# Projection to B and C in four column groups of the array, and one transpose of its result

## The chip, the cores and the metric

The kernel runs on one core of a Trainium2 chip. The metric is the device time of one execution in microseconds (us). Three runs of the kernel before took 1530.69, 1531.29 and 1533.32 us; the median is 1531.29 us. Engines are named as the profile names them: PE (TensorE, matmul), PEld (its weight load), DVE (VectorE), ACT (ScalarE), POOL (GpSimd) and SP (the queue that issues DMAs).

## The reference, cut to what matters

The input is x with 2 sequences (B = 2) of 2048 steps and 256 features. A feed-forward layer comes first, then a state-space layer, then the same feed-forward layer again. The change is in the middle layer, in two of its small projections:

```
xc = silu(conv(x_branch))                     # (B, L, 512)
dt = soft_clamp(softplus(xc @ W_dt.T + b_dt))
Bp = xc @ W_B.T                               # (B, L, 16)
Cp = xc @ W_C.T                               # (B, L, 16)
# scan over L: h = h * exp(dt A) + dt * Bp * xc ;  y = sum_n h * Cp + D * xc
```

W_B and W_C have 16 rows each. The kernel keeps them side by side as one matrix `wbc` of 32 columns, so one projection gives 32 numbers a step: 16 of B and 16 of C.

## The kernel before, in words

There are three stages. The pre stage walks over 8 tiles; a tile is 256 steps of both sequences, 512 columns (4 blocks of 128, G = 4, two for each sequence). It runs the first feed-forward layer of the next tile, and the projections and the convolution of the current one, and writes its results to DRAM. The scan stage walks over blocks of 10 steps for both sequences, and the post stage computes the output and the last feed-forward layer.

All work is written out by hand: each engine has its own list, and semaphores tie the lists together. In the pre stage four PSUM banks form a ring. PE fills a bank, ACT reads it, and the list `order` says which result has which place (`fill` on PE, `held` on ACT).

For tile i the lists run as follows.

- PE: `turn_zn(i)` (L346), `project_bc(i-1)` (L369), `project(i, "x")` (L353, after a wait for both ACT copies `copy_z`, L445), `turn_b(i-1)` (L378), `up(i+1)` (L314), `turn_xn(i+2)` (L304), `project(i, "gate")` (L353 again, which needs ring banks that the gelu L432 reads), `down(i+1)` (L328), `project_dt` (L361) with `turn_y(i+1)` (L338) in it.
- ACT: `copy_z` (L445), `copy_bc(i-1)` (L490), `copy_x` (L452), `copy_bt(i-1)` (L987), gelus of tile i+1 (L432), `silu_xc` (L461), `silu_gate` (L469), and softplus and tanh for dt.
- DVE: statistics, `apply1(i+2)` (L582, needs the rstd of POOL L257), the convolution (L642, L645, L650; its first operations need `copy_x`), `split_g(i+1)` (L602, L604), `low_x`, `residual(i+1)` (L612, needs `turn_y(i+1)`), `dt_u`, `apply2`.
- POOL: `norm2(i+1)` (L265 to L277), `spread_b(i-1, 2, 4)` (L1004), `rstd1(i+3)` (L257), then `spread_b(i, 0, 2)` (L995, L997, L1004), which needs `copy_bt`.
- SP: store r (L181), load x (L174), `store_bc` (L187), `store_b` (L1014), store xc, sg, dt and u (L138).

The projection to B and C is computed with the 32 columns of `wbc` as weights. Sequence 0 goes to PSUM partitions 0 to 31 and sequence 1 to partitions 32 to 63, so two groups of 32 array columns are in use. ACT copies the 64 x 256 result to `bcs`. SP stores it to DRAM for the C part, and PE turns it (two transposes of 64 rows) for the B part.

Of the kernel before, what the change touches and what calls it, by code (L numbers as in the profile page):

```python
# [10 lines left out]
ACT = mybir.ActivationFunctionType  # L11
AX = mybir.AxisListType

P = 128
B, L, D = 2, 2048, 256
E = 512
N = 16
H = 1024
TAPS = 4
KD, KE, KH = D // P, E // P, H // P  # L20
TT = 256
TILES = L // TT
G = B * TT // P
# [6 lines left out]
CT = CB * S  # L30
# [20 lines left out]
def pre_stage(nc, dram, w, areas, banks, sem):  # L51
# [7 lines left out]
    own, first, second = areas  # L59
# [19 lines left out]
    xc = second.put("xc", [P, 2, KE, COLS])  # L79
# [1 line left out]
    dt_place = second.offset  # L81
    dt = second.put("dt", [P, KE, COLS])
    u = second.put("u", [P, KE, COLS])
    bcs = second.put("bcs", [B * 2 * N, TT])
    wbc = own.put("wbc", [P, KE, 2 * N])
    convw = own.put("convw", [P, KE, TAPS])
    convb = own.put("convb", [P, KE])
# [19 lines left out]
    ring_done, ring_read = sem("ring_done"), sem("ring_read")  # L107
# [6 lines left out]
    r_out, sg_out, bc_out, dt_out, u_out = (sem(n) for n in ("r_out", "sg_out", "bc_out", "dt_out", "u_out"))  # L114
# [19 lines left out]
    def steps(i):  # L134
        return bass.ds(i * TT, TT)

    def store(sp, name, tile, done, i):
        sp.dma_start(dram[name][:, :, steps(i)],  # L138
                     tile.rearrange("p a (b t) -> p (a b) t", b=B)).then_inc(done, 16)

    def store_dt_u(sp, i):
        sp.wait_ge(dt_ready, i + 1)
        store(sp, "dt", dt[:], dt_out, i)
        sp.wait_ge(u_ready, i + 1)
        store(sp, "u", u[:], u_out, i)
# [23 lines left out]
    def sync(sp, scan, post):  # L169
        def load_x(i, *batches):  # L170
            if i >= XT:
                sp.wait_ge(x1_ready, i - XT + 1)
            for b in batches:
                sp.dma_start(xt[:, i % XT, 2 * b:2 * b + 2, :],  # L174
                             dram["x"][b, steps(i), :].rearrange("(h p) d -> p h d", p=P)
                             ).then_inc(x_in[i % XT], 16)

        def store_r(i):
            sp.wait_ge(r_ready, G * (i + 1))
            for b in range(B):  # L180
                sp.dma_start(dram["r"][b, steps(i), :].rearrange("(h p) d -> p h d", p=P),  # L181
                             r[:, 2 * b:2 * b + 2, :]).then_inc(r_out, 16)

        def store_bc(i):
            sp.wait_ge(ring_read, use["bc", i, 0] + 1)
            for b in range(B):
                sp.dma_start(dram["bc"][:, b, steps(i)], bcs[b * 2 * N:(b + 1) * 2 * N]).then_inc(bc_out, 16)  # L187

        load_x(0, 0)
        sp.dma_start(raw1[:, 0], dram["w1T"][0:P]).then_inc(raw1_in, 16)  # L190
        sp.dma_start(w1n[:, 0:4], dram["w1"][0:H // 2].rearrange("(m p) k -> p m k", p=P)).then_inc(w1n_in, 16)
        load_x(1, 0, 1)
        sp.dma_start(w.b1[:], dram["b1"]).then_inc(b_in, 16)
        sp.dma_start(raw2, dram["w2T"].rearrange("(k p) d -> p k d", p=P)).then_inc(raw2_in, 16)
        sp.dma_start(w.b2[:], dram["b2"]).then_inc(b_in, 16)
        sp.dma_start(w2n, dram["w2"].rearrange("(k p) h -> p k h", p=P)).then_inc(w2n_in, 16)
        for dst, src in ((win[:], dram["winT"].rearrange("(k p) m -> p k m", p=P)),
                         (convw[:], dram["convw"]), (convb[:], dram["convb"]),
                         (normw[:], dram["normw"]), (bdt[:], dram["bdt"]),
                         (wdt[:], dram["wdtT"].rearrange("(k p) m -> p k m", p=P)),  # L200
                         (wbc[:], dram["wbcT"].rearrange("(k p) m -> p k m", p=P))):
            sp.dma_start(dst, src).then_inc(p_in, 16)
        load_x(2, 0, 1)
        sp.wait_ge(pad_zero, 1)
        n = LP - L
        zero = pad[:].rearrange("p a c -> p (a c)")[:, 0:KE * B * n].rearrange("p (a c) -> p a c", c=n)
        sp.dma_start(dram["dt"][:, :, L:LP], zero).then_inc(padded, 16)
        sp.dma_start(dram["u"][:, :, L:LP], zero).then_inc(padded, 16)
        sp.dma_start(dram["bc"][:, :, L:LP], zero[0:2 * N, 0:B, :]).then_inc(padded, 16)
        for b in range(B):  # L210
            sp.dma_start(dram["ub"][b, L:L + S].rearrange("t v x -> (t v) x"),
                         pad[0:S * SPLITS].rearrange("p a c -> p (a c)")[:, 0:ROW]).then_inc(padded, 16)
        store_r(0)
        for i in range(TILES):
            if i + XT < TILES:
                load_x(i + XT, 0, 1)
            if i >= 1:
                store_bc(i - 1)
            if i in (6, 7):
                scan.load_piece(sp, i - 5)  # L220
                for half in range(2):
                    scan.store_piece(sp, i - 6, half)
            if i >= 2:
                scan.store_b(sp, i - 2, 2, G)
            if i >= 1:
                scan.store_b(sp, i - 1, 0, 2)
            sp.wait_ge(xc_ready, 2 * (i + 1))
            store(sp, "xc", xc[:, i % 2], xc_out[i % 2], i)
            sp.wait_ge(ring_read, use["gate", i, KE - 1] + 1)
            store(sp, "sg", sg[:], sg_out, i)  # L230
            if i >= 1:
                store_dt_u(sp, i - 1)
            if i == 4:
                scan.load_piece(sp, 0)
            if i < LAST:
                store_r(i + 1)
            else:
                scan.load_units(sp)
                scan.store_b(sp, LAST - 1, 2, G)
            if i == 3:  # L240
                post.load_params(sp)
                sp.wait_ge(padded, 80)
                scan.load_first(sp)
        store_bc(LAST)

    def gpsimd(pool, scan):
# [46 lines left out]
    def tensor(pe, scan):  # L293
        def fill(what):
            n = use[what]
            if n >= RING:
                pe.wait_ge(ring_read, n - RING + 1)
            return psR[:, n % RING, :]
# [66 lines left out]
        def project_bc(i):  # L365
            out = fill(("bc", i, 0))
            for k in range(KE):
                for b in range(B):
                    mm = pe.matmul(out[b * 2 * N:(b + 1) * 2 * N, 0:TT], wbc[:, k, :],  # L369
                                   xc[:, i % 2, k, b * TT:(b + 1) * TT], start=(k == 0), stop=(k == KE - 1))  # L370
            mm.then_inc(ring_done, 1)

        def turn_b(i):
            out = fill(("bt", i, 0))
            pe.wait_ge(ring_read, use["bc", i, 0] + 1)
            rows = B * 2 * N
            for x in range(TT // P):
                mm = pe.transpose(out[:, x * rows:(x + 1) * rows], bcs[:, x * P:(x + 1) * P], w.ident[0:rows, 0:rows])  # L378
            mm.then_inc(ring_done, 1)

        pe.wait_ge(consts, 1)
        turn_xn(0)
# [8 lines left out]
        for i in range(TILES):  # L391
# [19 lines left out]
            if i in (5, 6):  # L411
                scan.turn_piece(pe, i - 5, psD[:, 0], 0, KE)
        project_bc(LAST)
        turn_b(LAST)

    def scalar(act, scan, post):
        def held(what):
            n = use[what]
            act.wait_ge(ring_done, n + 1)
            return psR[:, n % RING, :]  # L420
# [62 lines left out]
        def copy_bc(i):  # L483
            src = held(("bc", i, 0))
            if i == LAST:
                act.wait_ge(ring_read, use["bc", i, 0])
            if i >= 1:
                act.wait_ge(bc_out, 16 * B * i)
                act.wait_ge(ring_done, use["bt", i - 1, 0] + 1)
            act.activation(bcs[:], src[0:B * 2 * N, 0:TT], ACT.Copy).then_inc(ring_read, 1)  # L490

        def copy_bt(i):
            src = held(("bt", i, 0))
# [288 lines left out]
def scan_stage(nc, dram, w, areas, banks, sem, pre):  # L782
# [9 lines left out]
    own, first, second = areas  # L792
    dtc = own.put("dtc", [P, 2, KE * B, DB * S])
    bc = [own.put(f"bc{q}", [P, B, N, S]) for q in range(RING)]
# [4 lines left out]
    bt = own.put("bt", [P, G, N])  # L799
# [61 lines left out]
    def tile_of(t):  # L861
        return min(t // TT, TILES - 1)
# [1 line left out]


    def relayout(sp, c):
        sp.wait_ge(pre.bc_out, 16 * B * (tile_of((c + 1) * CT) + 1))
        for b in range(B):
            sp.dma_start(
                dram["blk"][c * CB:(c + 1) * CB, b, :, :].rearrange("k n t -> n k t"),  # L870
                dram["bc"][N:2 * N, b, c * CT:(c + 1) * CT].rearrange("n (k t) -> n k t", t=S)
            ).then_inc(blk_out, 16)
# [111 lines left out]
    def copy_bt(act, i, src, read):  # L984
        if i >= 1:
            act.wait_ge(b_split, 2 * i)
        act.activation(bt[:].rearrange("p (b x) n -> p x b n", b=B),  # L987
                       src.rearrange("p (x b n) -> p x b n", b=B, n=2 * N)[:, :, :, 0:N], ACT.Copy).then_inc(read, 1)

    def spread_b(pool, i, q0, q1):  # L990
        if q0 == 0:
# [886 lines left out]
```

## Time and profile before

| | |
|---|---|
| median of 3 runs | 1531.29 us |
| profiled execution, own time | 1536.68 us |
| its span | 1534.8 us |
| PE busy | 1455.1 us (95%) |
| DVE busy | 1255.2 us (82%) |
| ACT busy | 1121.2 us (73%) |
| POOL busy | 939.6 us (61%) |
| pre stage, roughly | 0 to 420 us |
| scan stage, roughly | 420 to 1330 us |
| post stage, roughly | 1330 to 1535 us |

Busy time counts an engine while an instruction of it runs. A row of the timeline gives the start, the time over which a group of instructions ran, the engine and line, what is written and read, the count, and in brackets the idle time before the group and what ended it. A busy share of 95% is a mean over stages; whether a shorter instruction shortens a stage is seen only in the waits of that stage.

### The profile page before, as it was taken

To read this page: it belongs to the slowest core of one execution; us is meant where nothing else is said; L and a number is where in the kernel's file an instruction comes from. 1 tells how busy PE (TensorE), PEld (TensorE's weight loads), DVE (VectorE), ACT (ScalarE), POOL (GpSimd) and SP (SyncE) were. 2 spreads that over 40 slices of the span, in tenths; PEclk is the share of its full clock that TensorE was granted. 3 is DMA by queue.
4 is the path that set the end of the run, shared out by engine and by line. 5 is a ranking of instruction groups with operands and counts; after the bars stand their busy time and mean duration, and the time that the engine had idled before them with its cause. 6 is when DMAs were issued, how large, how long until landed. Compare 5 with 4: busy or idle time off the path is not lost.

```text
span 1534.8 us, 25461 instructions
## 1 busy us (share of the span) xinstructions
PE 1455.1 (95%) x6902; PEld 1020.6 (66%) x6902; DVE 1255.2 (82%) x2526; ACT 1121.2 (73%) x2618; POOL 939.6 (61%) x956
## 2 busy tenths in 40 slices
PE   6999999999979999999999999999999998999998
PEld 5555555555467777777777777777666666677776
DVE  6685566745479999999999999999999998788884
ACT  4444455455999999999999999999999964334243
POOL 0224313432269999999999999999999997400000
PEclk9999999999999999999999999999999999999999
DMA  8215437453757667666666666666545447466420
GB/s 269 83 49 176 131 103 198 139 178 115 233 137 208 169 165 188 168 172 167 172 165 181 177 162 181 157 173 172 133 111 112 95 105 224 116 221 193 150 84 28
DMA packets 231557, 236.28 MB, mean 154 GB/s; under 512 B 46040, under 2 KB 197272, under 8 KB 231416
## 3 DMA queue, kind: packets, MB, share of 16 engines
q1 hardware_dynamic: 230472, 233.34, 54.4%
q8 instruction: 58, 0.95, 0.3%
q10 hardware_dynamic: 944, 1.31, 0.2%
q14 instruction: 83, 0.68, 0.2%
HBM read 136.31 MB, written 98.56 MB: 153 GB/s over the span
## 4 chain that ended last, share of the span: by engine, by line
DVE 35%; POOL 14%; PE 12%; issue 5%; DVEq 1%; POOLq 1%; DMA 1%; ACT 0%; SPq 0%; ACTq 0%
DVE h L1346 22%; POOL rc L1110 13%; DVE banks L1336 8%; PE banks L1495 4%; PE banks L1516 3%; PE banks L1526 3%; DVE qs L1330 2%; PE banks L1170 1%; DVEq L1344 1%; DMA ub<-scratch_ub 1%; DVE q_ln_st L1772 1%; DVE q_g L1681 1%; POOLq L1118 1%; DVE q_x L1653 1%; PE banks L1536 0%
## 5 line engine op out<-in xcount | busy, mean ns | idle before, releaser
L1346 DVE TENSOR_TENSOR_SCAN h<-decay,banks 128x352 f32<-128x352 f32 x820 | 710.4, 882 | 57.4 <-DVE banks L1336 2.9
L1121 POOL TENSOR_TENSOR hc<-h,bc 128x640 f32<-128x640 f32 x410 | 593.3, 1447 | 0.0
L1170 PE MATMUL banks<-hc,w_ident 128*128 128x320 f32 (+1 forms) x1664 | 526.6, 440 | 0.1
L1239 ACT ACTIVATE tb<-dtc,a 128x320 f32<-128x320 f32 (+1 forms) x832 | 417.2, 555 | 4.8 <-DVE x L612 4.8
L1170 PEld LDWEIGHTS banks<-hc,w_ident 128*128 128x128 f32 x1664 | 285.0, 191 | 70.7 <-issue 0.8
L1261 ACT ACTIVATE decay<-tb 128x640 f32<-128x640 f32 x410 | 294.9, 723 | 0.0
L1110 POOL TENSOR_TENSOR rc<-qs,w_mhalf 128x1 f32<-128x1 f32 x410 | 225.8, 551 | 110.5 <-DVE qs L1330 110.5
L1156 PE MATMUL banks<-ub 128*128 128x176 f32 x1640 | 273.5, 289 | 2.4 <-DMA ub<-scratch_ub 2.4
L1149 PEld LDWEIGHTS banks<-sc_ss,sc_ones 128*128 128x128 f32 x820 | 123.5, 189 | 158.2 <-ACT sc_sq L1250 152.2
L1156 PEld LDWEIGHTS banks<-ub 128*128 128x128 f32 x1640 | 217.6, 193 | 2.6 <-DMA ub<-scratch_ub 2.6
L1149 PE MATMUL banks<-sc_ss,sc_ones 128*128 128x1 f32 x820 | 151.8, 254 | 37.7 <-ACT sc_sq L1250 19.5
L1250 ACT ACTIVATE sc_sq<-h 128x64 f32<-128x64 f32 x410 | 128.3, 313 | 76.7 <-issue 47.4
L1336 DVE TENSOR_SCALAR banks<-h,rc 128x64 f32<-128x64 f32 x410 | 137.2, 335 | 3.6 <-POOL rc L1110 2.0
L265 POOL TENSOR_TENSOR ln_rz<-ln_vz,w_mhalf 128x4 f32<-128x4 f32 x8 | 13.9, 1734 | 202.7 <-DVE ln_vz L618 202.7
L353 PE MATMUL banks<-zT,win 128*128 128x512 f32 x256 | 118.8, 618 | 9.6 <-ACT gf L432 8.6
L361 PE MATMUL banks<-xc,wdt 128*128 128x512 f32 x256 | 114.0, 599 | 3.4 <-ACT sg L469 3.4
L1482 POOL TENSOR_TENSOR q_ln_rs<-q_ln_ve,w_mhalf 128x4 f32<-128x4 f32 x8 | 10.9, 1365 | 170.7 <-DVE q_ln_ve L1777 170.7
L1583 ACT ACTIVATE q_gf<-banks,w_b,w_a 128x512 f32<-128x512 f32 x64 | 49.9, 780 | 69.6 <-PE banks L1516 67.7
L353 PEld LDWEIGHTS banks<-zT,win 128*128 128x128 f32 x256 | 49.0, 196 | 71.1 <-issue 59.0
L361 PEld LDWEIGHTS banks<-xc,wdt 128*128 128x128 f32 x256 | 48.7, 193 | 59.8 <-issue 55.0
L612 DVE TENSOR_TENSOR x<-banks,xt 128x1024 f32<-128x1024 f32 x8 | 9.8, 1225 | 84.3 <-PE banks L338 84.3
L432 ACT ACTIVATE gf<-banks,w_b,w_a 128x512 f32<-128x512 f32 x64 | 48.3, 778 | 39.6 <-DVE g L604 31.4
(133 smaller groups left out, 1818.5 us busy)
## 6 DMA issues: line engine op xcount, KB each, us to landing
ub<-scratch_ub SPq DMA_DIRECT2D x410, 107.5 KB
bc<-scratch_blk SPq DMA_DIRECT2D x205, 160.0 KB, 3.5
scratch_ub<-turned SPq DMA_DIRECT2D x64, 512.0 KB, 3.6
scratch_ub<-spread SPq DMA_DIRECT2D x64, 176.0 KB, 2.6
scratch_xc<-xc SPq DMA_DIRECT2D x8, 1024.0 KB, 4.8
scratch_sg<-sg SPq DMA_DIRECT2D x8, 1024.0 KB, 6.0
piece<-scratch_u SPq DMA_DIRECT2D x32, 256.0 KB, 4.0
q_ys<-scratch_y SPq DMA_DIRECT2D x8, 1024.0 KB, 5.7
```

The lines of the kernel that those rows point to most:

```text
L353: mm = pe.matmul(out, win[:, k, (m0 + m) * P:(m0 + m + 1) * P], zT[:, k, :], start=(k == 0), stop=(k == KD - 1))
L361: mm = pe.matmul(out, wdt[:, k, m * P:(m + 1) * P], xc[:, i % 2, k, :], start=(k == 0), stop=(k == KE - 1))
L1110: pool.tensor_tensor(rc[:, b:b + 1], qs[:, b:b + 1], w.mhalf[:, 0:1], ALU.pow).then_inc(norm_ready, 1)
L1121: pool.tensor_tensor(hc[:, pl % 2, :, at * S:(at + 1) * S] .rearrange("p (c b n) e -> p c b n e", c=KE, b=B)[:, :, b], state(m)[:, :, 0:S] ...
L1149: pe.matmul(psQ[:, b:b + 1], ones[:], ss[:, b:b + 1], start=True, stop=True).then_inc(sum_ready, 1)
L1156: mm = pe.matmul(psI[m % B][:, c * N * W:(c + 1) * N * W], ub[m % URING][:, c * P:(c + 1) * P], ub[m % URING][:, E:], start=True, stop=True)
L1170: mm = pe.matmul(banks[:, y_bank(p), 0:KE * B * wide], w.ident[:], rhs, start=(n == 0), stop=(n == N - 1))
L1239: act.activation(tanh_rows(c, r), dtc[:, c % 2, k * B:(k + 1) * B, 0:blocks_of(c) * S].rearrange("p b (k e) -> p k b e", e=S), ACT.Tanh, s ...
L1250: act.activation(sq[:, b, :], state(m - B)[:, :, S], ACT.Square, accum_out=ss[:, b:b + 1]).then_inc(sq_ready, 1)
L1261: act.activation(decay[:, m % DRING].rearrange("p (g i e) -> p g i e", g=DB, e=W)[:, :, :, 1:], tanh_block(j, b), ACT.Exp, scale=DTA_HALF ...
L1336: dve.tensor_scalar(inp(m)[:, :, 0], state(m - B)[:, :, S], rc[:, b:b + 1], None, ALU.mult).then_inc(carry_ready, 1)
L1346: dve.tensor_tensor_scan(state(m).rearrange("p r e -> p (r e)")[:, half], decay[:, m % DRING, half], psI[m % B][:, half], 0.0, ALU.mult, A ...
```

## The change

Each 128-step block of a tile now has a group of 32 array columns of its own: block q goes to PSUM partitions 32q to 32q+31. There are 16 matmuls of 128 columns in place of 8 of 256 columns (each shows as two records in the trace, since float32 takes two). `bcs` becomes 128 x 128 in place of 64 x 256, the copy on ACT has this shape, the two transposes of 64 rows become one of 128 rows, and the result has its blocks in the order in which `bt` wants them. The store to DRAM takes four DMAs in place of two.

```
-    bcs = second.put("bcs", [B * 2 * N, TT])
+    bcs = second.put("bcs", [G * 2 * N, P])
...
             for b in range(B):
-                sp.dma_start(dram["bc"][:, b, steps(i)], bcs[b * 2 * N:(b + 1) * 2 * N]).then_inc(bc_out, 16)
+                for x in range(TT // P):
+                    q = b * (TT // P) + x
+                    sp.dma_start(dram["bc"][:, b, i * TT + x * P:i * TT + (x + 1) * P],
+                                 bcs[q * 2 * N:(q + 1) * 2 * N]).then_inc(bc_out, 16)
...
             for k in range(KE):
-                for b in range(B):
-                    mm = pe.matmul(out[b * 2 * N:(b + 1) * 2 * N, 0:TT], wbc[:, k, :],
-                                   xc[:, i % 2, k, b * TT:(b + 1) * TT], start=(k == 0), stop=(k == KE - 1))
+                for q in range(G):
+                    mm = pe.matmul(out[q * 2 * N:(q + 1) * 2 * N, 0:P], wbc[:, k, :],
+                                   xc[:, i % 2, k, q * P:(q + 1) * P], start=(k == 0), stop=(k == KE - 1))
...
-            rows = B * 2 * N
-            for x in range(TT // P):
-                mm = pe.transpose(out[:, x * rows:(x + 1) * rows], bcs[:, x * P:(x + 1) * P], w.ident[0:rows, 0:rows])
-            mm.then_inc(ring_done, 1)
+            pe.transpose(out[:, 0:P], bcs[:], w.ident[:]).then_inc(ring_done, 1)
...
-                act.wait_ge(bc_out, 16 * B * i)
+                act.wait_ge(bc_out, 16 * G * i)
...
-            act.activation(bcs[:], src[0:B * 2 * N, 0:TT], ACT.Copy).then_inc(ring_read, 1)
+            act.activation(bcs[:], src[:, 0:P], ACT.Copy).then_inc(ring_read, 1)
...
-        sp.wait_ge(pre.bc_out, 16 * B * (tile_of((c + 1) * CT) + 1))
+        sp.wait_ge(pre.bc_out, 16 * G * (tile_of((c + 1) * CT) + 1))
...
-        act.activation(bt[:].rearrange("p (b x) n -> p x b n", b=B),
-                       src.rearrange("p (x b n) -> p x b n", b=B, n=2 * N)[:, :, :, 0:N], ACT.Copy).then_inc(read, 1)
+        act.activation(bt[:], src.rearrange("p (q n) -> p q n", n=2 * N)[:, :, 0:N], ACT.Copy).then_inc(read, 1)
```

PE's list at the start of tile 1, before (a row is a line of the kernel, what it writes and reads, the shape of the result, and how often):

```order
L346 MATMUL banks<-w_ident,zn 128x128 x8
L369 MATMUL banks<-xc,wbc 32x256 x8
L353 MATMUL banks<-zT,win 128x512 x8
L378 MATMUL banks<-w_ident,bcs 128x64 x2
L314 MATMUL banks<-xT,w_s_49 128x512 x32
```

And with the change, where lines after the stores stand three further down:

```order
L349 MATMUL banks<-w_ident,zn 128x128 x8
L372 MATMUL banks<-xc,wbc 32x128 x16
L356 MATMUL banks<-zT,win 128x512 x8
L379 MATMUL banks<-w_ident,bcs 128x128
L317 MATMUL banks<-xT,w_s_49 128x512 x32
```

The place of every group in the list is kept; the group for B and C has twice the matmuls with half the columns, and two transposes became one.

SP's list in the same stretch (a later tile), before:

```order
L181 DMA scratch_r<-r 128x2x256 x2
L174 DMA xt<-in_x 128x2x256 x2
L187 DMA scratch_bc<-bcs 32x256 x2
L1014 DMA scratch_ub<-spread 256x1x176 x8
L138 DMA scratch_xc<-xc 1024x1x256
```

And with the change:

```order
L181 DMA scratch_r<-r 128x2x256 x2
L174 DMA xt<-in_x 128x2x256 x2
L189 DMA scratch_bc<-bcs 32x128 x4
L1013 DMA scratch_ub<-spread 256x1x176 x8
L138 DMA scratch_xc<-xc 1024x1x256
```

Two more issues stand ahead of the eight stores of `spread`.

## Rows read from the trace of the kernel before

**Rows 1.** Windows: busy us of each engine, PEclk, DMA share, GB/s.

```profile
87.40:370.00 282.60, 273.97 (x973) 159.30 (x972) 178.89 (x362) 147.12 (x202) 82.92 (x80) 0.99 0.47 142
```

**Rows 2.** Timeline of PE, 135 to 186 us: start, us, engine, line, count, idle before.

```profile
135.54 1.04 PE L346 MATMUL banks<-w_ident,zn 128*128 128x128 f32 x8
136.51 1.92 PE L369 MATMUL banks<-xc,wbc 128*32 128x256 f32 x16
138.36 7.13 PE L353 MATMUL banks<-zT,win 128*128 128x512 f32 x16
145.42 0.33 PE L378 MATMUL banks<-w_ident,bcs 64*128 64x64 f32 x2
145.69 7.76 PE L314 MATMUL banks<-xT,w_s 128*128 128x512 f32 x32
153.28 1.03 PE L304 MATMUL banks<-w_ident,xn 128*128 128x128 f32 x8
155.94 7.13 PE L353 MATMUL banks<-zT,win 128*128 128x512 f32 x16 [1.62 <-ACT gf L432]
...
173.84 1.04 PE L338 MATMUL banks<-w_ident,yT 128*128 128x128 f32 x8
```

**Rows 3.** Timeline of DVE, in tile 2, tile 1 and tile 4.

```profile
125.44 1.22 DVE L612 TENSOR_TENSOR x<-banks,xt 128x1024 f32<-128x1024 f32 x1 [11.26 <-PE banks L338]
...
141.32 1.38 DVE L582 TENSOR_SCALAR xn<-xt,ln_mv,ln_rs 128x256 f32<-128x256 f32 x4 [5.63 <-POOL ln_rs L257]
...
148.44 5.17 DVE L645 SCALAR_TENSOR_TENSOR cv<-xbuf,convw,cv 128x512 f32<-128x512 f32 x6
...
92.09 0.55 DVE L642 TENSOR_SCALAR cv<-xbuf,convw,convb 128x512 f32<-128x512 f32 x1 [0.76 <-ACT xbuf L452]
...
247.31 4.05 DVE L645 SCALAR_TENSOR_TENSOR cv<-xbuf,convw,cv 128x512 f32<-128x512 f32 x6
```

**Rows 4.** Timeline of POOL, in tile 2 and tile 4.

```profile
140.25 1.04 POOL L257 TENSOR_TENSOR ln_rs<-ln_ve,w_mhalf 128x4 f32<-128x4 f32 x1
...
148.31 2.10 POOL L1004 TENSOR_TENSOR spread<-bts,mask 128x352 fp32r<-128x352 f32 x2
...
259.62 1.27 POOL L1004 TENSOR_TENSOR spread<-bts,mask 128x352 fp32r<-128x352 f32 x1 [12.51 <-DMA scratch_ub<-spread]
```

**Rows 5.** Timeline of ACT, tile 2.

```profile
136.33 1.26 ACT L445 ACTIVATE zT<-banks,normw 128x512 f32<-128x512 f32 x2
138.47 0.38 ACT L490 ACTIVATE bcs<-banks 64x256 f32<-64x256 f32 x1 [0.89 <-PE banks L369]
...
146.02 0.22 ACT L987 ACTIVATE bt<-banks 128x64 f32<-128x64 f32 x1
...
155.11 0.78 ACT L432 ACTIVATE gf<-banks,w_b,w_a 128x512 f32<-128x512 f32 x1 [4.59 <-DVE g L604]
```

**Rows 6.** Waits of PE, 80 to 340 us: total us, times, longest.

```profile
PE banks L353 <- ACT gf L432: 6.5, 5, 1.6
```

**Rows 7.** Timeline of PE, after other waits.

```profile
253.69 7.13 PE L353 MATMUL banks<-zT,win 128*128 128x512 f32 x16 [0.46 <-ACT gf L432]
...
352.70 8.83 PE L353 MATMUL banks<-zT,win 128*128 128x512 f32 x16 [2.14 <-ACT gf L432]
...
404.55 4.84 PE L361 MATMUL banks<-xc,wdt 128*128 128x512 f32 x7 [3.36 <-ACT sg L469]
...
424.56 0.31 PE L378 MATMUL banks<-w_ident,bcs 64*128 64x64 f32 x2 [2.60 <-ACT bcs L490]
...
1285.60 1.16 PE L1156 MATMUL banks<-ub 128*128 128x176 f32 x4 [2.08 <-DMA ub<-scratch_ub]
```

**Rows 8.** Windows after two of these waits; the eighth number is PEclk.

```profile
352.70:361.00 8.30, 8.30 (x17) 3.60 (x17) 6.32 (x13) 7.08 (x9) 0.00 (x0) 0.79 0.08 27
...
1285.00:1292.00 7.00, 6.40 (x19) 4.95 (x20) 4.33 (x8) 2.21 (x7) 3.00 (x3) 0.51 0.67 223
```

**Rows 9.** Timeline of SP's queue, tile 2.

```profile
140.80 1.00 SPq L187 DMA_DIRECT2D scratch_bc<-bcs  x2
141.85 9.91 SPq L1014 DMA_DIRECT2D scratch_ub<-spread  x8
```

## The prediction, made before the changed kernel ran

> **What bounds the kernel now.** I looked first at the windows by stage. The change touches only the pre stage, and there PE is busy for 274.0 of 282.6 us [rows 1]. That looks like a stage in which each microsecond taken from PE is a microsecond of the kernel. The timeline of PE says otherwise [rows 2]: in each tile it runs without a gap up to the gate projection, and there it waits for a gelu of ACT, 1.62 us in tile 2. In tiles 1 to 5 this wait comes five times, 6.5 us in all [rows 6].
>
> So I followed the wait back through the other engines. The gelu at 155.11 waited for DVE's split [rows 5], which stands behind the convolution in DVE's list. DVE came to the convolution late, because at 141.32 it had waited 5.63 us for POOL's rstd [rows 3, 4]. POOL works off a list that begins with statistics of DVE's residual at 125.44, and that residual waited for PE's `turn_y` [rows 3]. From `turn_y` on 173.84 the round starts again. The loop that sets the period is therefore: PE from the gate projection to `turn_y` (155.94 to 173.84, 17.90 us), DVE residual, POOL, DVE convolution and split, ACT gelu, PE gate. The projection to B and C and the turn (L369, L378) lie on PE between `turn_y` and the gate, beside DVE and POOL, and not in the loop. The 1.62 us are their slack.
>
> **The projection on PE.** The x projection puts 16 records of 512 columns between 138.36 and 145.42, 0.44 us each [rows 2]; so 256 columns by themselves need 0.22. But the 16 records of L369, 256 columns each, fill only 136.51 to 138.36: 0.116 us each. Two run side by side, one in each group of columns, in 8 steps. With the change there are 32 records of 128 columns. The best case is four side by side, 8 steps. A step of 128 columns with a full weight load takes (136.51 - 135.54) / 8 = 0.12 in L346 [rows 2], and four loads of 32 columns are as much weight as one of 128; so 8 x 0.12 = 0.97 us, and PE is ready at 137.48. The worst cases are two side by side (16 steps, 1.9 us, as now) and none (32 steps, 3.9 us). I take four, since two groups already overlap fully.
>
> The Trainium skill speaks for it too: TensorEngine Tiling (Array Packing), section Overview, has up to four times the rate for 32 columns. By that full factor the sum would be as I have it; at two groups the trace agrees with its factor of two, and no row shows four.
>
> The x projection waits for ACT's two copies, done at 136.33 + 1.26 = 137.59 [rows 5]. A release takes about 0.05 us (gelu end 155.89, gate start 155.94), so L353 starts at 137.64 and not at 137.48: it gains 0.72 of the possible 0.88 us.
>
> **The turn.** Two transposes of 64 rows hold PE from 145.42 to 145.69 [rows 2]; one of 128 x 128 is a step of 0.12. It saves 0.15. PE then comes to the gate 0.72 + 0.15 = 0.87 us earlier.
>
> **What that is worth.** In tiles 2, 3, 4 and 5 DVE and POOL are not released by anything that moved, so the gate starts when it did and the wait grows by 0.87: to 2.5 in tiles 2, 3 and 5, to 1.3 in tile 4 (0.46 before [rows 7]). Gain: nothing. In tile 1 DVE did wait for the x copy at 92.09 [rows 3], and in tile 6 likewise (it has no `apply1`). There the convolution, the split and the gate come 0.72 us earlier: 2 x 0.72 = 1.44 us gained. The wait of tile 6 grows only by 0.15, from 2.14 to 2.3.
>
> **ACT.** The copy to `bcs` has 128 columns in place of 256. Rows of 256 and 64 columns take 0.38 and 0.22 [rows 5], so 128 take about 0.27, 0.1 less. ACT is the bound around 390 us and again before the first scan at 424 us (PE waits for it there [rows 7]): 2 x 0.1 = 0.2 us. The copies of the six other tiles are in ACT's idle time. The copy of `bt` reads as many elements and is kept.
>
> **SP.** Two more issues a tile, 0.5 us each as the two in [rows 9], put the first stores of `spread` from 141.85 to 142.8. POOL's next use of that buffer is at 148.31 [rows 4], and moves up with `bt` to 147.6 or so. The fourth store is issued by 145.3, and I bound its landing at 3 us: 148.3, which is about when the second spread starts. Cost between 0 and 0.5 us of POOL time off the loop; I take 0.
>
> **DVE against POOL.** In tile 2 the last six convolution steps took 5.17 us, in tile 4 they took 4.05 [rows 3]. The difference is that in tile 2 POOL spread B at 148.31 meanwhile, and in tile 4 it did so only at 259.62 [rows 4]. So the spreads cost the loop 1.12 us a tile. The Trainium skill has this rule (SBUF — State Buffer, Who interferes with whom): a VectorE instruction with two SBUF inputs and a GpSimd instruction that reads SBUF exclude each other. By that rule the cost depends only on whether they overlap; the sum would change only if the spreads left the convolution. The convolution lasts to 153.6 and the spreads move by under 1 us, so I keep 1.12 on both sides, with 0.1 us a tile either way.
>
> **The clock.** The expensive part is what the longer waits do. In tile 6 PE had waited 2.14 us, and the gate projection then took 8.83 in place of 7.13 us [rows 7, 2]. Its granted clock was 0.79 in that stretch [rows 8]: it fell to the lower level, 1.2 GHz, for a while. That is in the loop, and it cost 1.70 us. The same happened after the waits of 2.08 us (clock 0.51 [rows 8]), 2.60 and 3.36 us [rows 7]. After none of the waits of 1.6 us did it: 7.13 us each. So, once the kernel is past its start, four of four waits over 2 us were followed by a fall, and none of those in tiles 1 to 5. The change takes three waits over that line, in tiles 2, 3 and 5, to 2.5 us. I count a fall for each: 3 x 1.70 = 5.10 us. The bounds are 0 (no further fall) and about 3.4 us each, if the lower level lasts as long as after the wait of 2.08 (7 us). I take 1.70, the row of the same place.
>
> **Sum.** +5.10 - 1.44 - 0.2 = +3.46 us. On the profiled execution's own 1536.68 this gives 1540.1; that execution is 5.4 us over the median of the runs, and for a new median the sum goes on 1531.29: 1534.7 us, or 0.23% slower. A measurement of this kernel tells a difference from none at about 0.2%, 3.1 us, so this is just beyond the edge.
>
> **Rivals.**
>
> *No further fall, a small gain.* The three longer waits don't lower the clock; what was seen in tile 6 was bad luck. For it: only one of the four falls is at this very place. Against it: all waits over 2 us had one. Then -1.44 - 0.2 gives 1529.7 us, not slower, and from 2.5 us waits with a clock of 1.00 behind them one would know it.
>
> *Four groups don't run side by side.* Two at a time give 1.9 us as now, and only the turn gets shorter; waits grow to 1.8 us, no fall, 1531.1 us. One at a time adds 2 us a tile; the slack hides it in tiles 2, 3 and 5, while tiles 1, 4 and 6 pay 2, 1.5 and 2 us: 1536.8 us. For it: no row has four. Against it: two do overlap fully.
>
> *The spreads leave the convolution.* If SP's longer list held the stores of `spread` back as it did in tile 4, the convolution would be 1.1 us shorter in up to four tiles. With the small gain that is 1525.3 us, faster. It decides only if the landing comes some 5 us later than now; the two issues are 1 us.
>
> **How the numbers follow.** The forecast has 0.58; with two to four new falls it lies between 1533 and 1536.4, so 0.37 of it is slower by over 0.2% and 0.21 within. No further fall has 0.24 (0.19 within, 0.05 faster). The missing overlap has 0.14 (0.11 within, 0.03 slower). The spreads have 0.04, faster. Together: faster 0.09, same 0.51, slower 0.40. The range reaches from 1529.3, the small gain, to 1537, where a fall of longer length or the missing overlap would lie; 0.04 lies below and some 0.08 above, besides what the runs scatter.
>
> **What the profile will show.** If I am right: the B and C projection has 32 records in about 1.1 us; L353 (then L356) starts 1.1 us after it and behind a short wait for `zT`; the waits for the gelu are 2.5 us in tiles 2, 3 and 5; the gate projection after them takes 8 to 9 us with a clock well below 1; and DVE's residuals lie about 51 us apart there in place of 49.5. The gate waits with 7.13 us behind them would refute the clock step. A projection that still takes 1.9 us would refute the overlap. Residuals 0.7 us closer in tiles 2 to 5 would refute the loop.

## The result, and the profile after

The changed kernel takes 1533.51 us (median of 20 runs, 1531.01 to 1536.98) against 1529.66 us of the kernel before (20 runs, 1527.68 to 1534.73). The ratio is 1.0023 with a 95% interval of 1.0014 to 1.0032: slower by 0.23%. (Ratios here and below are formed from all the runs of both kernels; they are close to the quotient of the two medians and not equal to it.) In the profiles PE is busy for 10.8 us less (1444.3 us in place of 1455.1), and the kernel is 3.9 us slower.

The profiled execution of after took 1533.52 us, span 1531.6. That of before had 1536.68, some 7 us over its later median, so the two spans can't be subtracted. From DVE's first residual (near 35 us) to its second one (near 75 us) before spent 41.0 us and after 38.4, because the clock of before was low near 46 us; and from the last residual to the end of the span before took 1.6 us longer. The tiles between can be compared, and the table does it below.

PE's timeline of after in tile 2 answers to [rows 2]; L372 is the projection to B and C, L379 the turn, L317 and L356 are L314 and L353 of before:

```profile
131.72 1.04 PE L349 MATMUL banks<-w_ident,zn 128*128 128x128 f32 x8
132.68 1.08 PE L372 MATMUL banks<-xc,wbc 128*32 128x128 f32 x32
133.81 7.13 PE L356 MATMUL banks<-zT,win 128*128 128x512 f32 x16
140.78 0.27 PE L379 MATMUL banks<-w_ident,bcs 128*128 128x128 f32 x1
140.81 7.74 PE L317 MATMUL banks<-xT,w_s 128*128 128x512 f32 x32
```

The 32 records run for 1.08 us where 16 ran for 1.92, and L356 starts 1.13 us after them in place of 1.85: 0.72 gained. It waits for ACT, not for the projection, as the timeline of PE's weight loads shows:

```profile
132.68 0.81 PEld L372 LDWEIGHTS banks<-xc,wbc 128*32 128x32 f32 x32 [0.16 <-ACT v L476]
133.81 0.30 PEld L356 LDWEIGHTS banks<-zT,win 128*128 128x128 f32 x2 [0.32 <-ACT zT L445]
```

The load ahead of L356 stood for 0.32 us until `zT` was there. The turn costs 0.03 in place of 0.27 us (start of L379 to start of L317), and it starts 6.97 us behind the start of L356 in place of 7.06. From the start of the x projection to the start of `up` PE therefore needs 7.00 us in place of 7.33: 0.33 gained.

The copies on ACT, against [rows 5]:

```profile
132.50 1.26 ACT L445 ACTIVATE zT<-banks,normw 128x512 f32<-128x512 f32 x2
133.83 0.28 ACT L490 ACTIVATE bcs<-banks 128x128 f32<-128x128 f32 x1
```

0.28 in place of 0.38 us. Now PE's waits for the gelu, against [rows 6]:

```profile
PE banks L356 <- ACT gf L432: 11.0, 5, 2.7
```

From 6.5 to 11.0 us over five tiles: what PE saved, it waits. In tile 2 the wait is 2.67 in place of 1.62 us, 1.05 us longer, which is the 0.72 and the 0.33 us together. And what follows these waits, against [rows 7]:

```profile
152.09 7.13 PE L356 MATMUL banks<-zT,win 128*128 128x512 f32 x16 [2.67 <-ACT gf L432]
...
201.49 8.83 PE L356 MATMUL banks<-zT,win 128*128 128x512 f32 x16 [2.63 <-ACT gf L432]
...
300.93 8.63 PE L356 MATMUL banks<-zT,win 128*128 128x512 f32 x16 [2.68 <-ACT gf L432]
...
351.15 8.83 PE L356 MATMUL banks<-zT,win 128*128 128x512 f32 x16 [2.51 <-ACT gf L432]
```

The windows behind them, with the clock as the number after the five engines, against [rows 8]:

```profile
152.10:158.60 6.50, 6.50 (x15) 2.94 (x16) 6.30 (x14) 5.69 (x8) 0.00 (x0) 1.00 0.00 0
201.50:209.80 8.30, 8.30 (x17) 3.61 (x17) 7.50 (x15) 7.48 (x11) 0.00 (x0) 0.79 0.01 2
300.90:309.20 8.30, 8.27 (x17) 3.79 (x17) 7.54 (x15) 7.44 (x10) 0.00 (x0) 0.81 0.01 2
351.20:359.50 8.30, 8.30 (x17) 3.61 (x17) 6.26 (x13) 7.08 (x9) 0.00 (x0) 0.79 0.09 29
```

Three gate projections, in tiles 3, 5 and 6, ran partly at the lower level, 1.2 GHz, and took 1.5 to 1.7 us longer. Before, only tile 6 did. In tile 2 a wait of 2.67 us had no such consequence.

One more wait has grown, in tile 7, ahead of the projection to dt: 4.43 us, where [rows 7] have 3.36.

```profile
402.88 15.67 PE L364 MATMUL banks<-xc,wdt 128*128 128x512 f32 x32 [4.43 <-ACT sg L469]
```

In these two profiles the projection behind it takes about the same (15.57 us before). In those of two kernels of the experiments with a wait of this length it takes more: 16.67 us behind 4.44 (filled) and 16.96 behind 4.22 (half k).

The convolution is as long as before: its second half took 5.17 us beside the spreads, as in [rows 3].

```profile
144.59 5.17 DVE L645 SCALAR_TENSOR_TENSOR cv<-xbuf,convw,cv 128x512 f32<-128x512 f32 x6
```

SP's four stores take 1.85 us in place of 1.00, against [rows 9]:

```profile
137.21 1.85 SPq L189 DMA_DIRECT2D scratch_bc<-bcs  x4
139.11 8.81 SPq L1013 DMA_DIRECT2D scratch_ub<-spread  x8
```

All of the change can be read from one number a tile: the distance between two starts of DVE's residual (`psN + xt`, L612), which PE's `turn_y` releases once in a round. Column i is from the residual in the list of tile i-1 to that of tile i, which holds the gate projection of tile i. The last column is from there to the end of the span. Two kernels of the experiments below are in it for comparison.

| kernel | 1 | 2 | 3 | 4 | 5 | 6 | rest |
|---|---|---|---|---|---|---|---|
| before | 49.05 | 49.48 | 49.43 | 48.31 | 49.47 | 51.25 (low) | 1161.4 |
| after | 48.33 | 49.44 | 51.11 (low) | 48.28 | 50.96 (low) | 50.42 (low) | 1159.8 |
| half k | 48.33 | 51.15 (low) | 51.11 (low) | 48.30 | 51.16 (low) | 48.70 | 1161.8 |
| filled | 48.33 | 49.45 | 49.41 | 48.28 | 49.46 | 48.72 | 1157.9 |

"Low" marks a gate projection at a lowered clock. Tiles 2 to 5 without it are equal to 0.04 us between before and after; with it they are 1.5 to 1.7 us longer. Tile 1 is 0.72 us shorter, tile 6 is 0.83 shorter (both low). So six tiles sum to 297.0 us before and 298.5 after: 1.5 us slower, with the clock costing 3.2 us more. This is less than the 3.9 us between the medians: two profiles are two executions, and in which of them the clock falls differs from one to the next.

### The profile page after: what moved, and what is told of

Read it like the earlier page. It is cut to its first block, busy times and chain, and to the rows that moved or that the text cites. A ratio compares the mean times of both kernels' runs of the same rounds, so it can differ in the third digit from the quotient of the medians.

```text
span 1531.6 us, 25717 instructions
## 1 busy us (share of the span) xinstructions
PE 1444.3 (94%) x7022; PEld 1018.4 (66%) x7022; DVE 1253.3 (82%) x2526; ACT 1119.3 (73%) x2618; POOL 940.8 (61%) x956
## 4 chain that ended last, share of the span: by engine, by line
DVE 36%; POOL 13%; PE 12%; issue 5%; DVEq 1%; POOLq 1%; DMA 1%; ACT 0%; SPq 0%; ACTq 0%
DVE h L1345 23%; POOL rc L1109 13%; DVE banks L1335 9%; PE banks L1494 4%; PE banks L1515 3%; PE banks L1525 3%; DVE qs L1329 2%; DVEq L1343 1%; PE banks L1169 1%; DVE q_ln_st L1771 1%; DMA ub<-scratch_ub 1%; DVE q_g L1680 1%; POOLq L1117 1%; DVE q_x L1652 1%; PE banks L1535 0%
## 5 line engine op out<-in xcount | busy, mean ns | idle before, releaser
L356 PE MATMUL banks<-zT,win 128*128 128x512 f32 x256 | 118.8, 619 | 14.8 <-ACT gf L432 13.6
L356 PEld LDWEIGHTS banks<-zT,win 128*128 128x128 f32 x256 | 49.2, 197 | 75.3 <-issue 56.4
L612 DVE TENSOR_TENSOR x<-banks,xt 128x1024 f32<-128x1024 f32 x8 | 9.8, 1224 | 85.0 <-PE banks L341 85.0
```

Source lines behind the costliest of these rows:

```text
L356: mm = pe.matmul(out, win[:, k, (m0 + m) * P:(m0 + m + 1) * P], zT[:, k, :], start=(k == 0), stop=(k == KD - 1))
```

## The experiments

Ratios are against the kernel before, run on the same chip in the same job, and have 95% intervals.

**Products that nobody reads, in the longer waits (after).** The theory is that the clock falls because PE has nothing to do in the wait. The rival is that something else in the change costs the time.

```
+        def fill_wait(i):
+            times = {2: 3, 3: 3, 5: 3, 6: 3}.get(i, 0)
...
+            for _ in range(times):
+                pe.matmul(psD[:, 0, 0:320], w.ident[:], w.s1[:, 0, 0:320].bitcast(F32), start=True, stop=True)
...
+            fill_wait(i)
             project(i, "gate", KE)
```

> The changed kernel, and ahead of the gate projection of tiles 2, 3, 5 and 6 PE computes three products of 320 columns into a PSUM bank that nobody reads (about 1.6 us in all), inside its wait of 2.5 to 2.7 us. Clock theory: the waits that are left are about 1.0 us, the granted clock stays full in these tiles, every gate projection takes 7.13 us and none 8.6 to 8.8. The changed kernel has three falls in its profile at 1.5 to 1.7 us each, so the time goes from 1533.5 to about 1528.5 us, 1 to 2 us under the kernel before. Rival (the slowdown comes from the stores, from the layout or from where POOL's work falls, and the clock is a bystander): work put into a wait changes nothing, 1533.5 us.

Measured: 1527.56 us (11 runs, 1526.45 to 1529.22), ratio 0.9979 (0.9970 to 0.9989). That is 2.7 us under the kernel before in the same job (1530.24), where the change by itself was 3.9 us over it: about 6 us under the changed kernel (1533.51). Its 11 runs scatter by 2.8 us, where the 20 of before and of after scatter by 6 to 7. In tile 3 the timeline has:

```profile
200.13 1.78 PE L388 MATMUL banks<-w_s,w_ident 128*128 128x320 f32 x6
202.91 7.13 PE L356 MATMUL banks<-zT,win 128*128 128x512 f32 x16 [1.01 <-ACT gf L442]
```

PE does 1.8 us more work in each of the four tiles, the wait is 1.01 us, the gate takes 7.13 us, and every tile is at its short length in the table. The clock theory holds; a rival in which the clock is a bystander can't give a gain by adding work. This kernel has the gains of the change without the price of it.

**The same in the kernel before, tile 6 alone.**

```
+            times = {6: 3}.get(i, 0)
...
+            for _ in range(times):
+                pe.matmul(psD[:, 0, 0:320], w.ident[:], w.s1[:, 0, 0:320].bitcast(F32), start=True, stop=True)
```

> The kernel before, with the same three products ahead of the gate projection of tile 6 alone, where PE waits 2.1 us. Clock theory: this wait of the kernel before lowers the clock in some executions and not in all; filled, it never does. So between 0 and 1.7 us faster than before, about 1 us in the middle (1528.7), and the scatter from run to run gets smaller. Rival (the clock is a bystander): no difference, or up to 0.1 us slower.

Measured: 1529.95 us, ratio 0.9994 (0.9984 to 1.0003). The sign is as expected and the size, 0.3 us where about 1 was in the middle of the expectation, too small to tell from none; tile 6 took 49.55 us in its profile. A smaller scatter was expected too, and isn't clear: 5.1 us over 11 runs, where the 11 of four stores, without a fill, have 6.1. The comparison can't decide alone, but it shows how little there is to win in the kernel before: the filled version of after is better by 2.4 us in the median.

**Half of the contraction left out (before).** The same PE time saved in another way, without layout, stores or new transpose.

```
-            for k in range(KE):
+            for k in range(KE // 2):
...
-                                   xc[:, i % 2, k, b * TT:(b + 1) * TT], start=(k == 0), stop=(k == KE - 1))
+                                   xc[:, i % 2, k, b * TT:(b + 1) * TT], start=(k == 0), stop=(k == KE // 2 - 1))
```

> The kernel before with two of the four blocks of the contraction left out in the projection to B and C: 8 records in place of 16, so PE gains about 0.93 us a tile by other means, while the layout, the two stores, the copy on ACT and the two transposes are those of before. Clock theory: the gate waits grow to 2.3 to 2.5 us as with the change, falls follow, and the time is 2 to 4 us over the kernel before (about 1533 us), with the gains of 0.72 us in tiles 1 and 6 in it. Rival (stores, layout or the new transpose cost the time): those are not here, so the time is 0 to 1.5 us under the kernel before (1528.2 to 1529.7).

Measured: 1535.15 us (12 runs) against 1530.24, ratio 1.0025 (1.0013 to 1.0037). Half of the work of this projection gone, and slower:

```profile
133.16 1.06 PE L369 MATMUL banks<-xc,wbc 128*32 128x256 f32 x8
134.28 7.13 PE L353 MATMUL banks<-zT,win 128*128 128x512 f32 x16
141.35 0.33 PE L378 MATMUL banks<-w_ident,bcs 64*128 64x64 f32 x2
141.61 7.76 PE L314 MATMUL banks<-xT,w_s 128*128 128x512 f32 x32
149.21 1.03 PE L304 MATMUL banks<-w_ident,xn 128*128 128x128 f32 x8
152.56 8.83 PE L353 MATMUL banks<-zT,win 128*128 128x512 f32 x16 [2.32 <-ACT gf L432]
```

A wait of 2.32 us, then 8.83 us for the gate; the same in tiles 3 and 5 (table). In tile 6 a wait of 2.15 us had 7.13 us behind it. It reproduces the result with none of the change's other parts, so the lost time comes from PE's shorter list and what that does to the clock.

The granted clock of each whole run says this over more executions than the profiles. Its mean is 0.9908 over the 20 runs of after and 0.9908 over the 12 of half k; it is 0.9942 over the 35 runs of before in the job of half k, and 0.9948 over the 11 of filled. A fall that costs 1.70 of 1531 us lowers this mean by 0.0011. So 0.0034 are about three falls more a run, an estimate that doesn't say where in the run they lie.

**Four stores (before).**

```
-                sp.dma_start(dram["bc"][:, b, steps(i)], bcs[b * 2 * N:(b + 1) * 2 * N]).then_inc(bc_out, 16)
+                for x in range(TT // P):
+                    sp.dma_start(dram["bc"][:, b, i * TT + x * P:i * TT + (x + 1) * P],
+                                 bcs[b * 2 * N:(b + 1) * 2 * N, x * P:(x + 1) * P]).then_inc(bc_out, 16)
```

> The kernel before with four stores of 128 steps in place of two of 256 in each tile, all else kept. Clock theory: SP's two extra issues (1 us a tile) are hidden, since the next user of the spread buffer comes later; gate waits stay at 1.6 us; the time is that of before within 0.5 us. Rival (the stores cost the time): the whole of the change's 3.5 us shows here, 1533 us.

Measured: 1531.34 us, ratio 1.0001 (0.9990 to 1.0012). The stores cost nothing that can be seen: the interval allows up to 1.8 us, not the 3.9 us of the change. Its profile also has a wait that kept the clock:

```profile
350.03 7.13 PE L355 MATMUL banks<-zT,win 128*128 128x512 f32 x16 [2.14 <-ACT gf L434]
```

The same wait of 2.14 us as in [rows 7] in the same tile, and here 7.13 us behind it. So a wait of this length lowers the clock in some executions and not in all.

**One column group after the other (after).**

```
-            for k in range(KE):
-                for q in range(G):
+            for q in range(G):
+                for k in range(KE):
```

> The changed kernel with the loop over the four column groups outside and that over the contraction inside, so that neighbours in PE's list use the same group and can't run side by side. Overlap theory: the 32 records take about 32 x 0.11 = 3.5 us in place of 1.08; the gate waits shrink by 2.4 us to about 0.2 in tiles 2, 3 and 5; no clock fall there; tiles 1 and 6 pay 1.7 us each against before through the x copies, tile 4 about 0.9; in all 1532 to 1535 us. Rival (the records don't overlap between groups at all and each is short by itself): still 1.1 us for the 32, falls as with the change.

Measured: 1533.39 us against 1531.68, ratio 1.0010 (1.0000 to 1.0020).

```profile
135.21 2.46 PE L372 MATMUL banks<-xc,wbc 128*32 128x128 f32 x32
137.60 7.13 PE L356 MATMUL banks<-zT,win 128*128 128x512 f32 x16
```

The order of the same 32 records makes 2.46 us of 1.08: the overlap of four groups is real, and it is full only where neighbours in the list are of different groups. In the trace of after the records start four at a time, within 20 ns, and the next four 0.11 us later. Here they start alone (8 records) or in pairs (12 pairs), so there is still overlap in part, and 2.46 us came where 3.5 was expected. The gate waits were 1.52 to 1.56 us in tiles 1, 2, 3 and 5, and no clock fell there. Only tile 6, with 2.51 us, was low. The time came out in the expected range, but with less cost in PE and gate waits of 1.5 in place of 0.2 us, not by the expected sum.

**The spreads moved out of the round (before and after).** If DVE and POOL set the round, taking 2.7 us out of it must be worth what PE's slack allows, and then what the change takes off PE, 0.87 us a tile by the forecast, must be worth its full size.

```
 # POOL
-            if i >= 1:
+            if 1 <= i < LAST:
+                pool.wait_ge(split_lo, KH * (i + 2))
+                scan.spread_b(pool, i - 1, 0, G)
+            if i == LAST:
                 scan.spread_b(pool, i - 1, 0, 2)
             if i + 1 < TILES:
                 norm2(i + 1)
-            if i >= 1:
+            if i == LAST:
                 scan.spread_b(pool, i - 1, 2, G)
...
 # SP
-            if i >= 2:
-                scan.store_b(sp, i - 2, 2, G)
-            if i >= 1:
+            if i == LAST:
                 scan.store_b(sp, i - 1, 0, 2)
...
             store(sp, "sg", sg[:], sg_out, i)
+            if 1 <= i < LAST:
+                scan.store_b(sp, i - 1, 0, G)
```

> The kernel before, with all four spreads of B of a tile moved in POOL's list to the time after DVE's last split of the tile (DVE waits for turn_y there), and their stores behind that of sg in SP's list, in tiles 1 to 6. Loop theory: the round over DVE and POOL loses the 1.57 us of the two spreads ahead of the rstd and the 1.12 us that two spreads cost the convolution; PE then bounds the pre stage, gate waits are near 0, a tile takes about 47.9 us, no clock fall in them. Gain about 1.1 + 1.6 + 1.6 + 0.5 + 1.6 + 1.1 and the fall of tile 6: 7 to 9 us, 1521 to 1523 us. Rival (PE bounds the stage already, the waits are noise): no gain.

> The same move in the changed kernel. Loop theory: now the 0.87 us that the change takes off PE in each tile are worth their full size, since PE bounds the stage; and with waits gone the clock stays up. A tile takes about 47 us; 4 to 6 us under the moved kernel of before, about 1517 us. Rival (the change's saving is worth nothing in any order of the work): the same time as the moved kernel of before.

Measured, on one chip with 1531.68 for the kernel before: 1527.01 us, ratio 0.9962 (0.9948 to 0.9976), for before moved; 1521.90 us, ratio 0.9930 (0.9916 to 0.9944), for after moved. The change is now worth 5.1 us, faster. A tile takes 48.0 us in the one and 47.28 in the other, the same from tile 1 to 5 to 0.02 us; over six tiles that is 288.4 against 284.0 us, 4.4 of the 5.1. No gate projection of either is at a lowered clock. The timeline of after moved shows the wait:

```profile
147.42 1.03 PE L310 MATMUL banks<-w_ident,xn 128*128 128x128 f32 x8
148.96 7.13 PE L359 MATMUL banks<-zT,win 128*128 128x512 f32 x16 [0.50 <-ACT gf L435]
```

The wait is 0.50 us in place of 2.67, and DVE's convolution is free of the spreads:

```profile
142.57 4.06 DVE L648 SCALAR_TENSOR_TENSOR cv<-xbuf,convw,cv 128x512 f32<-128x512 f32 x6
```

4.06 us in place of the 5.17 above. A tile gains 0.72 us by the change here, though, and not the 0.87 that was expected, because PE doesn't bound the tile alone: a wait of 0.50 us is left in tiles 1 to 5 (before moved has 0.16 or less there), and DVE's convolution waits in it for ACT's copy of the x projection.

```profile
137.22 0.55 DVE L645 TENSOR_SCALAR cv<-xbuf,convw,convb 128x512 f32<-128x512 f32 x1 [0.39 <-ACT xbuf L455]
```

So what reaches the tile is the 0.72 us by which the x projection starts earlier; what the turn saves goes into the wait.

Both gains over the kernel before are less than expected: 4.7 us in place of 7 to 9, and 1521.9 us in place of about 1517. Part of it is given back in tile 7, where the waits of PE for ACT got longer (5.52 us ahead of the projection to dt) and the clock stayed low for longer behind them:

```profile
389.51 16.68 PE L367 MATMUL banks<-xc,wdt 128*128 128x512 f32 x32 [5.52 <-ACT sg L472]
```

From the last residual to the first scan after moved needs 58.9 us, where after needs 56.8.

**Tile 7 filled as well, and the moved kernel again.**

```
+        def fill_last(times):
...
+            for _ in range(times):
+                pe.matmul(psD[:, 0, 0:320], w.ident[:], w.s1[:, 0, 0:320].bitcast(F32), start=True, stop=True)
...
+            if i == LAST:
+                fill_last(7)
             pe.wait_ge(xc_ready, 2 * (i + 1))
             project_dt(i, 0, 1)
...
         project_bc(LAST)
+        fill_last(4)
         turn_b(LAST)
```

> The changed kernel with the spreads moved, and in tile 7 PE computes seven products that nobody reads inside its wait of 5.5 us ahead of the projection to dt, and four inside its wait of 3.3 us ahead of the last turn. Clock theory: the projection to dt behind the wait takes about 14 us in place of 16.7, and part of that reaches the end, since ACT works beside it: 1 to 3 us under the moved kernel without it, about 1520 us. Rival (ACT alone bounds this stretch): no difference.

> The changed kernel with the spreads moved, once more, on the same chip as the one with tile 7 filled. Both theories: 9 to 11 us under the kernel before, as in the first run of it; it is the other half of the comparison.

Measured, with 1532.60 for the kernel before: 1519.72 us (6 runs, 1516.92 to 1529.20), ratio 0.9925 (0.9902 to 0.9948), with the fill, and 1521.59, ratio 0.9927 (0.9910 to 0.9944), without. The medians differ by 1.9 us, but the intervals are nearly the same, so the times don't tell the two apart. The profile shows the step itself:

```profile
385.84 3.93 PE L388 MATMUL banks<-w_s,w_ident 128*128 128x320 f32 x14
391.51 13.97 PE L367 MATMUL banks<-xc,wdt 128*128 128x512 f32 x32 [1.74 <-ACT sg L481]
```

13.97 us in place of 16.68 and 16.82 in the two profiles without the fill, and from the last residual to the first scan 56.7 us in place of 58.9 and 59.0. The four products ahead of the last turn did less: they left a wait of 1.58 us, and the clock fell behind it all the same.

```profile
412.00:419.00 7.00, 5.03 (x11) 3.49 (x12) 5.01 (x8) 6.97 (x17) 1.14 (x2) 0.51 0.35 100
```

This version, 0.75% under the kernel before by its ratio, has the lowest median of the study; the fill's own share of it is shown in the profile and not by the times.

## Why the prediction was right, step by step

- *The loop.* Right, to a few hundredths: tiles 2 to 5 kept 49.45 and 48.3 us where the clock stayed up. Moving the spreads confirms it from the other side: with 2.7 us of work taken out of DVE and POOL the tile went from 49.45 to 48.0 us, and PE had almost no wait left.
- *The projection.* Four groups side by side: 0.97 us forecast for 32 records, 1.08 measured from the first start to the last end; L356 gained 0.72, as forecast, and the rest is lost to the wait for `zT`. The turn was put at 0.15 us; with it PE saved 0.33, so it came to the gate 1.05 us earlier and not 0.87, and the waits are 2.6 to 2.7 us and not 2.5. In the rival of no overlap the slack of 1.62 us was said to hide the whole of 2.0 us; by its own numbers, with the 0.15 of the turn, some 0.2 us a tile would have been left.
- *Tiles 1 and 6.* 0.72 each forecast; 0.72 and 0.83 measured. The wait of tile 6 was to grow to 2.3 us and is 2.51.
- *ACT.* The copy is 0.28 us (0.27 forecast). Whether its 0.1 us reached the end isn't shown.
- *SP.* Nothing forecast, nothing measured (1.0001), and POOL's spreads of tile 2 (144.47 us) had no wait for a store ahead of them.
- *DVE against POOL.* Unmoved, 5.17 us on both sides.
- *The clock.* Three further falls were forecast at 1.70 us each, 5.10 in all. The profile has two further ones, at 1.68 and 1.49 us, 3.2 in all, and tile 2 had none. The reading of four falls behind four waits as a rule was too strong: of the gate waits over 2 us in the profiles of before, after, half k, four stores and one after the other, eight of eleven were followed by a fall, and none of those under 1.7 us. So the term is better read as a chance of about three in four for each wait, which gives 3.8 us for three in place of 5.1. The mean clock over all runs, lower by about three falls, speaks for a little more; it counts tile 7 too, whose longer wait the forecast had left out. Filling shows that the falls are the cause.
- *The sum.* +3.46 us forecast, +3.85 measured between the medians of 20 runs. The mechanism and the sign are shown, the closeness of the number is in part luck. The forecast counted a fall behind every long wait of after. Against that it carried the fall of tile 6 in every execution of before, and four stores, whose tile 6 has the same wait, shows that it isn't in all. By the two profiles alone the sum would be +1.5 us.

What stays open: which wait lowers the clock in a given execution, and why in the profile of after the one in tile 2 did not. Stretches at the lower level near 46 and 1285 us also come and go from profile to profile, and with them 1 to 3 us. There no such line between short and long waits shows: near 46 us five of the eleven profiles have the lower level behind the same waits of 1.7 and 1.0 us, and near 1280 us the clock fell behind waits of 1.24 us (before filled) and 1.55 us (four stores), and did not behind 1.51 us (tile 7 filled).

## What to carry to other kernels

An engine that is busy for 97% of a stage need not set its length: follow the one wait it has left back through the other engines until the chain closes, and price a saving only if it lies on that loop. A saving off the loop wasn't free here, since it lengthened TensorE's wait, and behind a longer wait the clock fell for work that is on the loop. Either shorten the loop together with it (here 5.1 us gained for the change, where alone it lost 3.9), or fill the wait with work.

## What the runs showed of the hardware beyond what was expected

- Adding 1.8 us of PE work a tile in four tiles made the kernel about 6 us faster (1533.51 to 1527.56).
- Four records of 32 columns each, one for each column group, start within 20 ns of each other, every 0.11 us. With one group after the other in the list, 32 records took 2.46 us, where single starts at 0.11 us would take 3.5: 24 of them started in pairs. That the two of a pair are of different groups is likely; the trace doesn't name the group.
- POOL's cast of B took 0.24 us outside DVE's convolution and 0.37 to 2.13 us inside it for the same 128 x 64 elements, and DVE lost nothing by it: the six steps beside it took 4.06 us with a cast of 1.38 us (before) and of 2.08 us (after). The two spreads behind it cost DVE 1.05 to 1.12 us in each tile in which they fell inside the convolution.
